# Tanh on features in PSUM, three banks for gate and up, the last three pairs pre-added, and new places

## The chip, the cores and the metric

The kernel runs on one core of one Trainium2 chip (trn2). The metric is the device time of one launch in microseconds (us), as the median of several runs. The core has TensorE (matrix products into PSUM), VectorE, ScalarE (one table function per instruction), GpSimd and SyncE; each engine works through its own instructions in order, and semaphores keep the engines apart.

## The reference

Two layers of a gated model on x (8 batches x 512 rows x 256 columns) and a context of 64 rows per batch. Cut to what matters:

```python
# layer 0: attention over 64 context rows, then a mixture of experts (8 experts, the best 2 of each row, and a shared one)
x = x + tanh(g_xattn[0]) * attention(layernorm(x), ctx, side)
x = x + tanh(g_ffn[0]) * (expert(ln, shared) + sum_e cw[e] * expert(ln, e))   # expert: silu(x Wg) * (x Wu) @ Wd
# layer 1: additive attention, then a quantized linear layer
h   = tanh(txt_proj[:, None, :, :] + feat_proj[:, :, None, :] + b)            # 8 x 512 x 64 x 256
rho = einsum('bftd,d->bft', h, w)
att = softmax(rho masked); txt_h = att @ text
w_s, b_s = tanh(txt_h @ Wcw + bcw), tanh(txt_h @ Wcb + bcb)
x = x + tanh(g_xattn[1]) * (w_s * layernorm(x) + b_s)
x = x + tanh(g_ffn[1]) * (round_and_clip(layernorm(x) / s) * s @ (ternary - 1) + bias)
```

The Tanh over 8 x 512 x 64 x 256 elements is the largest work of ScalarE, the experts that of TensorE.

## The kernel before

**Stages.** First each batch goes through attention, normalization, routing and a scatter of its rows by expert into DRAM, while TensorE also works on the shared expert of batches 0 to 4 (units of kind shared). Then come 71 tiles of 128 routed rows and, among them, 12 tiles of kind own, which are the shared expert on the rows of batches 5 to 7. A tile, called a unit, has these steps: fetch (SyncE loads its rows and 1.5 MB of weights), turn_rows (TensorE transposes the rows), gate and up (TensorE, a PSUM bank each), gate_act (ScalarE's Silu of gate, then VectorE's product with up, which gives act), narrow (TensorE, into bank 5, which VectorE copies out). From the moment that a batch's rows are complete, they are gathered, added to x and normalized (mix_in), and TensorE makes two products feature(b, 0) and feature(b, 1), one for each half of the 256 columns, 128 x 512 each.

**Pairs.** For each batch there are 32 pairs (b, m), each of two text rows. A pair needs Tanh of the features plus a text column, 2 x 2 times 128 x 512 elements. A pair is either done alone, in four ScalarE instructions that add the text column as bias (L748), or it is added first: VectorE makes the four sums (preadd, L1124 and L1125) and ScalarE runs one Tanh of 2048 columns (L737). PAIRS says how many of a batch's 32 pairs are added. On some pairs, as many as JOINS says, VectorE folds the lower half into the upper (join, L1131), and TensorE's sum of the pair (L1484, 32 output columns, into bank 6) has half as many products. Eight pair buffers rotate: a pair's buffer is free when the sum of the pair eight before is done. After 32 pairs, mix_out: rho is read, turned, softmaxed, and the linear layer follows (turn_q, linear 0 and 1).

**Order.** Each stage has a place on a common line of time units: a batch's 32 pairs take 64 units, a routed tile 8, a pair 2. Each engine's order is by place plus its own lag from LAGS. PLACES holds the places of chains, as "opened", the listing of which tiles are opened (a chain of small VectorE instructions, L1018 to L1035), of sum, join and preadd. Only the order follows from it; the times are what semaphores make of it. The tail is what comes after the last tile, from the middle of batch 6 on.

**Banks.** Gate and up of unit n stand in banks 2(n%2) and 2(n%2)+1, the shared expert's narrow in bank 4, rows in 5, rho in 6. All other products rotate through a pool (function count): banks 7, 5 and 6 while routing runs, 7 and 4 among the tiles, more in the tail. The features are among these: VectorE copies them from their bank to featT in SBUF (L1114), and before it does so it waits for the last Tanh of the batch before that reads featT. Preadd and the alone Tanhs read featT:

```python
read = [m for m in range(T // 2) if b and not plan.added(b - 1, m)]
if read:
    e.wait_ge(s_wide, pair_of(b - 1, read[-1]) + 1)
...
e.tensor_copy(featT[ec], bank[:, :]).then_inc(done, 1)
```

Line numbers of the rows: L1287 gate and up, L1292 those of the shared expert, L1411 turn_rows, L1458 narrow, L1466 feature, L1484 sum, L1516 linear, L1386 turn_odds on TensorE; L728 Silu of gate, L667 copies out of PSUM, L718 and L699 work of routing on ScalarE; L1242 linear, L958 sigmoid on VectorE.

## Time and profile before

| | |
|---|---|
| time, median of 3 runs | 1027.43 us (1023.06 to 1028.69) |
| profiled execution, span | 1025.4 us |
| TensorE (PE) busy | 934.7 us, 91% |
| its weight loads (PEld) | 742.7 us, 72% |
| VectorE (DVE) busy | 748.9 us, 73% |
| ScalarE (ACT) busy | 674.1 us, 66% |
| GpSimd (POOL) busy | 219.0 us, 21% |
| moved by DMA | 218.68 MB, mean 213 GB/s |

The span is that of the profiled execution, from its first to its last instruction; the time of a run is measured from outside. How to read it: busy shares are means over stages with different limits. ScalarE is 66% busy in all but almost idle up to 360 us. A matmul's end is modelled, so a busy TensorE need not be at its peak; what tells more is whether one group of matmuls starts as the one before ends. In a group "x24" 24 records stand together; an f32 product is recorded as two.

### The profile page before, as it was taken

To read this page: it belongs to the slowest core of one execution; us is meant where nothing else is said; L and a number is where in the kernel's file an instruction comes from. 1 tells how busy PE (TensorE), PEld (TensorE's weight loads), DVE (VectorE), ACT (ScalarE), POOL (GpSimd) and SP (SyncE) were. 2 spreads that over 40 slices of the span, in tenths; PEclk is the share of its full clock that TensorE was granted. 3 is DMA by queue.
4 is the path that set the end of the run, shared out by engine and by line. 5 is a ranking of instruction groups with operands and counts; after the bars stand their busy time and mean duration, and the time that the engine had idled before them with its cause. 6 is when DMAs were issued, how large, how long until landed. Compare 5 with 4: busy or idle time off the path is not lost. (4 is left out here: it accounts for less than half of the span.)

```text
span 1025.4 us, 22330 instructions
## 1 busy us (share of the span) xinstructions
PE 934.7 (91%) x8078; PEld 742.7 (72%) x8078; DVE 748.9 (73%) x1959; ACT 674.1 (66%) x983; POOL 219.0 (21%) x250
## 2 busy tenths in 40 slices
PE   8689999989988799999999999999999999985773
PEld 5557887779988787777777878888888887842331
DVE  3787988862222389978869869868876997795995
ACT  2122222201100069999999999989997998899992
POOL 1014543540112222312212211202211211220000
PEclk9579999999998899999999999999999999989886
DMA  7826677948996866756756667768777776410000
GB/s 247 338 62 236 244 267 283 351 174 279 331 338 227 272 232 226 236 165 219 237 175 228 211 202 253 267 219 277 266 253 231 268 260 220 149 32 12 2 22 21
DMA packets 137456, 218.68 MB, mean 213 GB/s; under 512 B 14113, under 2 KB 79138, under 8 KB 137346
## 3 DMA queue, kind: packets, MB, share of 16 engines
q1 hardware_dynamic: 119202, 156.55, 45.9%
q10 hardware_dynamic: 8592, 34.60, 8.7%
q0 software_dynamic: 9552, 26.10, 7.2%
q8 instruction: 65, 1.06, 0.4%
q14 instruction: 45, 0.37, 0.1%
HBM read 159.14 MB, written 58.06 MB: 212 GB/s over the span
## 5 line engine op out<-in xcount | busy, mean ns | idle before, releaser
L1287 PE MATMUL bank<-rowsT,expert_w 128*128 128x128 f32 x2656 | 328.3, 278 | 0.5 <-DVE rowsT L1053 0.5
L1287 PEld LDWEIGHTS bank<-rowsT,expert_w 128*128 128x128 f32 x2656 | 319.1, 194 | 9.5 <-issue 5.1
L748 ACT ACTIVATE tanhs<-shared_w,txtT 128x512 f32<-128x512 f32 x276 | 174.3, 718 | 24.5 <-issue 18.4
L748 ACT ACTIVATE arena<-shared_w,txtT 128x512 f32<-128x512 f32 x272 | 172.1, 720 | 0.0
L1458 PE MATMUL bank<-expert_w,act 128*128 128x256 f32 x664 | 162.4, 388 | 0.0
L1458 PEld LDWEIGHTS bank<-expert_w,act 128*128 128x128 f32 x664 | 121.7, 193 | 30.6 <-issue 17.3
L728 ACT ACTIVATE act<-bank 128x512 f32<-128x512 f32 x83 | 48.9, 589 | 114.2 <-PE bank L1287 114.2
L643 POOL DMA_DIRECT2D rows_by_expert<-rows_out x71 | 42.0, 592 | 371.4 <-DVE rows_out L1082 349.2
L654 POOL DMA_INDIRECT picked<-rows_by_expert,slot_of x64 | 75.9, 1186 | 157.6 <-issue 93.9
L1484 PE MATMUL bank<-arena,pick_w 128*32 128x256 f32 x1200 | 79.2, 389 | 3.2 <-ACT arena L737 2.3
L1484 PE MATMUL bank<-tanhs,pick_w 128*32 128x256 f32 x1112 | 74.4, 412 | 7.3 <-ACT tanhs L737 4.7
L1082 DVE COPY rows_out<-bank 128x256 f32<-128x256 f32 x71 | 29.8, 420 | 68.8 <-PE bank L1458 68.8
L633 POOL DMA_INDIRECT rows_by_expert<-arena,slot_of x64 | 63.2, 987 | 69.7 <-DVE slot_of L1003 53.2
L1292 PE MATMUL bank<-tanhs,shared_w 128*128 128x256 f32 x320 | 77.8, 392 | 0.0
L1131 DVE SCALAR_TENSOR_TENSOR tanhs<-tanhs,ratio 128x1024 f32<-128x1024 f32 x53 | 67.1, 1278 | 1.8 <-ACT tanhs L748 1.8
L1292 PEld LDWEIGHTS bank<-tanhs,shared_w 128*128 128x128 f32 x320 | 60.7, 197 | 9.9 <-issue 2.2
L748 ACT ACTIVATE normT<-shared_w,txtT 128x512 f32<-128x512 f32 x96 | 61.4, 721 | 0.0
L1484 PEld LDWEIGHTS bank<-tanhs,pick_w 128*32 128x32 f32 x1112 | 34.2, 117 | 37.0 <-issue 8.7
L1484 PEld LDWEIGHTS bank<-arena,pick_w 128*32 128x32 f32 x1200 | 35.6, 111 | 32.9 <-ACT arena L737 6.9
L1060 DVE TENSOR_TENSOR act<-act,bank 128x512 f32<-128x512 f32 x83 | 56.3, 678 | 1.6 <-ACT act L728 1.6
L1104 DVE SCALAR_TENSOR_TENSOR x<-picked,share,x 128x256 f32<-128x256 f32 x64 | 30.7, 480 | 34.6 <-DMA picked<-rows_by_expert,slot_of 33.8
L1053 DVE COPY rowsT<-bank 128x256 f32<-128x256 f32 x83 | 34.8, 419 | 28.1 <-PE bank L1411 28.0
(257 smaller groups left out, 1392.1 us busy)
## 6 DMA issues: line engine op xcount, KB each, us to landing
expert_w<-in_WgT SPq DMA_DIRECT2D x71, 512.0 KB, 3.9
expert_w<-in_WuT SPq DMA_DIRECT2D x71, 512.0 KB, 5.2
expert_w<-in_WdT SPq DMA_DIRECT2D x71, 512.0 KB, 6.9
rows_by_expert<-tanhs ACTq DMA_DIRECT2D x8, 4096.0 KB, 14.3
rows_in<-rows_by_expert SPq DMA_DIRECT2D x71, 128.0 KB, 6.1
rows_by_expert<-rows_out POOLq DMA_DIRECT2D x71, 128.0 KB, 5.6
expert_w<-in_WgsT SPq DMA_DIRECT2D x12, 512.0 KB, 3.8
expert_w<-in_WusT SPq DMA_DIRECT2D x12, 512.0 KB, 4.6
```

Source lines behind the costliest of these rows:

```text
L633: e.indirect_dma_start(out=rows_dram, out_offset=bass.IndirectOffsetOnAxis(ap=slot_of[j][:, ST * b + i:ST * b + i + 1], axis=0), in_=held[ ...
L643: e.dma_start(rows_dram[bass.ds(tile * P, P), :], rows_out[r % OUTS][:, :]).then_inc(s_stored[r % OUTS], 16)
L654: e.indirect_dma_start(out=picked[u % PICKED][:, :], out_offset=None, in_=rows_dram, in_offset=bass.IndirectOffsetOnAxis(ap=slot_of[j % 2] ...
L728: e.activation(act[n % 2][:, :], banks[2 * (n % 2)][:, :], ACT.Silu).then_inc(s_tanh, 1)
L748: got = e.activation(tiles[ec][:, S * j:S * (j + 1)], featT[ec], ACT.Tanh, bias=txtT[:, ec, t + j:t + j + 1])
L1053: e.tensor_copy(rowsT[r % 2][:, :], row_bank[:, 0:D]).then_inc(s_row_bank, 1)
L1060: e.tensor_tensor(h[:, :], h[:, :], bu[:, :], ALU.mult).then_inc(s_h, 1)
L1131: e.scalar_tensor_tensor(out=high, in0=low, scalar=ratio[:, 0:1], in1=high, op0=ALU.mult, op1=ALU.add).then_inc(s_joined, 1)
L1287: got = e.matmul(bank[:, i * P:(i + 1) * P], w[:, at:at + P], t[:, c * P:(c + 1) * P], start=c == 0, stop=c == DC - 1)
L1292: got = e.matmul(bank[:, i * HALF:(i + 1) * HALF], shared_w[:, at:at + P], norm_of(b)[:, c * S + h * HALF:c * S + (h + 1) * HALF], start=c ...
L1458: got = e.matmul(row_bank[:, 0:D], act[n % 2][:, c * P:(c + 1) * P], w[:, at:at + D], start=c == 0, stop=c == IC - 1)
L1484: got = e.matmul(rho_bank[32 * j:32 * j + 32, 0:H], pick_w[:, ec, 31 - m:63 - m], halves_of[q % PAIR][ec][:, j * H:(j + 1) * H], start=(ec ...
```

## The change

ScalarE's alone Tanhs read the features in PSUM, in banks 3 and 4 (feat_bank), where TensorE writes them; VectorE still copies them to featT, for the preadds, and the new semaphore s_feat counts these copies. Both the preadds and a batch's first alone Tanh wait for it. TensorE's feature product waits for the copy of the batch before and for that batch's last alone Tanh; VectorE's copy no longer waits for Tanhs. To free bank 3, gate and up of the tiles rotate through banks 0 to 2: unit n's up takes the bank that gate of n-1 had, and waits for that unit's Silu. Among the tiles all other products but the features use bank 7 alone. In batches 0 to 6 the last three pairs are always added, and PAIRS counts over the other 29. PAIRS, JOINS, PLACES and LAGS have new numbers. What is computed doesn't change. The diff, with the tables of lags cut:

```diff
--- before.py
+++ after.py
@@ -33,33 +33,38 @@
 
 ENGINES = ("sync", "gpsimd", "scalar", "vector", "tensor")
 
-PLACES = {"shared": -2.5, "zeroed": 62.5, "gap": 0, "opened": 25.5, "att_norm": 120, "att_norm_long": 30.5, "attend": 90,
-          "attend_long": 23.5, "moe_norm": 62, "moe_norm_long": 28, "route": 28, "route_long": 34, "late": -59, "gather": 4.5,
-          "norm": 2, "add": 7, "mix_in_end": -0.5, "join": 6.5, "sum": 5, "preadd": 4, "mix_out": 9.5, "mix_out_end": 49}
-
-
-PAIRS = {0: 18, 1: 9, 2: 12, 3: 0, 4: 0, 5: 0, 6: 13, 7: 27}
-JOINS = {0: 16, 1: 8, 2: 6, 3: 28, 4: 24, 5: 28, 6: 1, 7: 0}
+PLACES = {"shared": -2.5, "zeroed": 85, "gap": 0, "opened": 34, "att_norm": 120, "att_norm_long": 30.5, "attend": 90,
+          "attend_long": 23.5, "moe_norm": 62, "moe_norm_long": 28.5, "route": 28.5, "route_long": 33.5, "late": -59.5,
+          "gather": 2.5, "norm": 4, "add": 7, "mix_in_end": -0.5, "join": 7, "sum": 6, "preadd": 3, "mix_out": 10,
+          "mix_out_end": 48.5}
+
+
+LAST = 3
+PAIRS = {0: 16, 1: 6, 2: 6, 3: 0, 4: 0, 5: 0, 6: 11, 7: 28}
+JOINS = {0: 16, 1: 11, 2: 11, 3: 27, 4: 27, 5: 27, 6: 1, 7: 0}
 
 
 WARM = {"start": 14, "turn_rho": 2, "turn_q": 4, "linear": 0}
 
 
 LAGS = {
-    "sync": {"fetch": -21, "load_side": -5.5, "narrow": 0.5},
...
-    "scalar": {"gate_act": 1, "soft_rho": -0.5, "softmax": -1, "spread": -2, "squash": 2, "tanh": 1, ("turn", "att"): -0.5,
...
-               ("aggr", "moe"): -0.5, "apply": 2.5, "choice": -1, "convert": -16.5, "gate_act": 2.5, "join": -1, "larger": -9,
-               "linear": 3.5, "narrow": 1.5, ("newton", "att"): -2, ("newton", "lin"): -1.5, ("newton", "mix"): 0.5,
-               ("newton", "moe"): 1, "opened": 1.5, "pads": -1, "place": -0.5, ("power", "att"): -0.5, ("power", "lin"): 1,
...
-    "tensor": {"count": 2, "feature": -0.5, "larger": -2, "logits": -2.5, "narrow": 0.5, "scores": -1.5, "spread": 3, "sum": -1,
-               "text": -1, ("turn", "att"): -1, "turn_e": -3.5, "turn_rho": -3, "up": -1, "weigh": -0.5},
+    "sync": {"fetch": -16.5, "keep": 11, "linear": 4.5, "load_late": -9, "load_shared": 16, "load_side": -6.5, "load_x": -2.5,
...
+    "scalar": {"gate_act": -0.5, "logits": -2.5, "soft_rho": -0.5, "softmax": -0.5, "spread": -3, "squash": 2, "tanh": 1.5,
...
+               "apply": 1, "convert": -16.5, "count": -1, "feature": 1.5, "gate_act": 2.5, "join": -1, "larger": -7,
+               "linear": 3.5, "logits": -4, "narrow": 1.5, ("newton", "att"): -2.5, ("newton", "lin"): 1.5,
+               ("newton", "mix"): 0.5, ("newton", "moe"): 1, "opened": 0.5, "pads": -1, "place": -1, ("power", "att"): -1,
...
+    "tensor": {"convert": 1, "count": 2, "feature": 0.5, "larger": -2, "linear": 3, "logits": -1.5, "narrow": 0.5,
+               "scores": -1.5, "spread": 3, "sum": -1, "tiles": -1, ("turn", "att"): 0, ("turn", "mix"): -1, "turn_e": -1,
+               "turn_odds": 0.5, "turn_q": 0.5, "turn_rho": -4, "weigh": -0.5},
 }
 
 
@@ -175,8 +180,13 @@
 
     def added(self, b, m):
 
-        pairs, share = self.T // 2, int(PAIRS[b])
-        return m * share // pairs != (m + 1) * share // pairs
+        last = LAST if b < self.B - 1 else 0
+        pairs, share = self.T // 2 - last, int(PAIRS[b])
+        return m >= pairs or m * share // pairs != (m + 1) * share // pairs
+
+    def alone(self, b):
+
+        return [m for m in range(self.T // 2) if not self.added(b, m)]
 
     def joined(self, b, m):
 
@@ -270,7 +280,7 @@
         self.shared_no.append(h)
         self.row_no = {s: i for i, s in enumerate(
             s for s in self.of["tensor"] if s[0] == "turn_rows" or s[0] == "narrow" and self.units[s[1]][0] != "shared")}
-        self.misc = {}
+        self.misc, self.feature_turn = {}, {}
         self.after_units, freed = {}, []
         turns, uses = 0, [0] * 8
         pool, at = [7, 0, 1, 2, 3, 4, 5, 6], -1
@@ -282,14 +292,17 @@
                 pool, at = [7, 5, 6], -1
                 self.before_shared = list(uses)
             if s[0] == "routed":
-                pool, at = [7, 4], -1
+                pool, at = [7], -1
                 self.before_routed = list(uses)
-                freed = [4]
             if s[0] == "tail":
-                pool, at = [7, 4, 0, 1, 2, 3, 5], -1
-                freed += [0, 1, 2, 3, 5]
+                pool, at = [7, 0, 1, 2, 5], -1
+                freed += [0, 1, 2, 5]
             own = expand.get(s[0], [s] if s[0] in users or s[0] == "turn" else [])
             for u in own:
+                if u[0] == "feature":
+                    turns += 1
+                    self.feature_turn[u[1:]] = turns
+                    continue
                 at += 1
                 bank = pool[at % len(pool)]
                 uses[bank] += 1
@@ -410,6 +423,16 @@
 
         banks = [ctx.enter_context(nc.psum_tensor(f"bank{i}", [P, 512], F32)) for i in range(8)]
         shared_bank, row_bank, rho_bank = banks[4], banks[5], banks[6]
+        feat_bank = banks[3:5]
+        FIRST = plan.shared_units
+
+        def gate_bank(n):
+
+            return banks[2 * (n % 2)] if n < FIRST else banks[2 * (n - FIRST) % 3]
+
+        def up_bank(n):
+
+            return banks[2 * (n % 2) + 1] if n < FIRST else banks[(2 * (n - FIRST) + 1) % 3]
 
 
         rows_dram = nc.dram_tensor("rows_by_expert", ((ABSENT + 8) * P, D), F32, kind="Internal").ap()
@@ -443,6 +466,7 @@
         s_shared_mm, s_x_shared = sem("shared_product"), sem("x_shared_added")
         s_added = sem("x_expert_added")
         s_wide_in, s_wide, s_sum = sem("wide_added"), sem("wide_tanh"), sem("rho_product")
+        s_feat = sem("features_copied")
         s_joined, s_larger, s_swapped = sem("wide_joined"), sem("larger_ready"), sem("features_swapped")
         s_rho, s_rho_sub, s_rho_e = sem("rho_read"), sem("rho_less_max"), sem("rho_exp")
         s_ws, s_squash, s_affine, s_applied = sem("weighed"), sem("squashed"), sem("affine_ready"), sem("x_affine")
@@ -725,9 +749,9 @@
                         else:
                             e.wait_ge(s_shared_mm, shared_no[n - 2] + 1)
                     if by_rows(n):
-                        e.activation(act[n % 2][:, :], banks[2 * (n % 2)][:, :], ACT.Silu).then_inc(s_tanh, 1)
+                        e.activation(act[n % 2][:, :], gate_bank(n)[:, :], ACT.Silu).then_inc(s_tanh, 1)
                     else:
-                        e.activation(act[n % 2][:, :], banks[2 * (n % 2)][:, :], ACT.Tanh, scale=0.5).then_inc(s_tanh, 1)
+                        e.activation(act[n % 2][:, :], gate_bank(n)[:, :], ACT.Tanh, scale=0.5).then_inc(s_tanh, 1)
                 elif name == "tanh":
                     b, m = k
                     q = pair_of(b, m)
@@ -736,16 +760,15 @@
                         e.wait_ge(s_wide_in, wide_in_no[b, DC - 1, m] + 1)
                         e.activation(wide_pair[q % PAIR], wide_pair[q % PAIR], ACT.Tanh).then_inc(s_wide, 1)
                     else:
-                        if m == 0:
+                        if m == plan.alone(b)[0]:
                             for ec in range(DC):
-                                bank, use, _ = misc["feature", b, ec]
-                                e.wait_ge(s_misc[bank], use)
+                                e.wait_ge(s_feat, DC * b + ec + 1)
                         if q >= PAIR:
                             e.wait_ge(s_sum, q - PAIR + 1)
                         t = b * T + 2 * m
                         for ec in range(DC):
                             for j in range(2):
-                                got = e.activation(tiles[ec][:, S * j:S * (j + 1)], featT[ec], ACT.Tanh, bias=txtT[:, ec, t + j:t + j + 1])
+                                got = e.activation(tiles[ec][:, S * j:S * (j + 1)], feat_bank[ec][:, :], ACT.Tanh, bias=txtT[:, ec, t + j:t + j + 1])
                         got.then_inc(s_wide, 1)
                 elif name == "soft_rho":
                     b, = k
@@ -918,7 +941,7 @@
                 elif name == "turn" and k[0] == "mix":
                     kind, b, h = k
                     if h == 0 and b:
-                        e.wait_ge(s_misc_mm, misc["feature", b - 1, 1][2])
+                        e.wait_ge(s_misc_mm, plan.feature_turn[b - 1, 1])
                     bank, done = product(("turn", *k))
                     e.tensor_copy(turned(mixT, h), bank[:, :].rearrange("p (i c n) -> p i c n", i=2, c=DC)).then_inc(done, 1)
                 elif name == "scores":
@@ -1053,7 +1076,7 @@
                     e.tensor_copy(rowsT[r % 2][:, :], row_bank[:, 0:D]).then_inc(s_row_bank, 1)
                 elif name == "gate_act":
                     n, = k
-                    h, bg, bu = act[n % 2], banks[2 * (n % 2)], banks[2 * (n % 2) + 1]
+                    h, bg, bu = act[n % 2], gate_bank(n), up_bank(n)
                     e.wait_ge(s_tanh, n + 1)
                     if by_rows(n):
                         e.wait_ge(s_up, n + 1)
@@ -1105,19 +1128,15 @@
                                            in1=xi, op0=ALU.mult, op1=ALU.add).then_inc(s_added, 1)
                 elif name == "feature":
                     b, ec = k
-                    bank, done = product(("feature", b, ec))
-                    read = [m for m in range(T // 2) if b and not plan.added(b - 1, m)]
-                    if read:
-                        e.wait_ge(s_wide, pair_of(b - 1, read[-1]) + 1)
-                    if wide_in_no and b and plan.added(b - 1, T // 2 - 1):
+                    e.wait_ge(s_misc_mm, plan.feature_turn[b, ec])
+                    if b:
                         e.wait_ge(s_wide_in, wide_in_no[b - 1, DC - 1, T // 2 - 1] + 1)
-                    e.tensor_copy(featT[ec], bank[:, :]).then_inc(done, 1)
+                    e.tensor_copy(featT[ec], feat_bank[ec][:, :]).then_inc(s_feat, 1)
                 elif name == "preadd":
                     b, ec, m = k
                     q = pair_of(b, m)
                     w = halves_of[q % PAIR][ec]
-                    bank, use, _ = misc["feature", b, ec]
-                    e.wait_ge(s_misc[bank], use)
+                    e.wait_ge(s_feat, DC * b + ec + 1)
                     if q >= PAIR:
                         e.wait_ge(s_sum, q - PAIR + 1)
                     t = b * T + 2 * m
@@ -1254,10 +1273,8 @@
                 if use > 1:
                     e.wait_ge(s_misc[bank], use - 1)
                 if key in plan.after_units:
-                    if bank in (0, 1, 2, 3):
+                    if bank in (0, 1, 2):
                         e.wait_ge(s_h, len(units))
-                    elif bank == 4:
-                        e.wait_ge(s_x_shared, 2 * OWN)
                     elif bank == 5:
                         e.wait_ge(s_row_bank, len(row_no))
                 return banks[bank]
@@ -1422,16 +1439,20 @@
                             e.wait_ge(s_shared_w, 48)
                         for h in range(2):
                             e.wait_ge(s_misc[misc["turn", "moe", g, h][0]], misc["turn", "moe", g, h][1])
-                    if n >= 2:
+                    if n in (FIRST, FIRST + 1):
+                        e.wait_ge(s_h, n)
+                    elif n >= 2:
                         e.wait_ge(s_h, n - 1)
                     else:
                         for i in (2 * n, 2 * n + 1):
                             if plan.before_shared[i]:
                                 e.wait_ge(s_misc[i], plan.before_shared[i])
-                    up_down(n, banks[2 * (n % 2)], 0, s_gate)
+                    up_down(n, gate_bank(n), 0, s_gate)
                 elif name == "up":
                     n, = k
-                    up_down(n, banks[2 * (n % 2) + 1], N1, s_up)
+                    if n > FIRST:
+                        e.wait_ge(s_tanh, n)
+                    up_down(n, up_bank(n), N1, s_up)
                 elif name == "narrow":
                     n, = k
                     kind, g, s, j = units[n]
@@ -1459,7 +1480,15 @@
                         got.then_inc(s_rows_mm, 1)
                 elif name == "feature":
                     b, ec = k
-                    bank = product(("feature", b, ec))
+                    bank = feat_bank[ec]
+                    if b:
+                        e.wait_ge(s_feat, DC * (b - 1) + ec + 1)
+                        if plan.alone(b - 1):
+                            e.wait_ge(s_wide, pair_of(b - 1, plan.alone(b - 1)[-1]) + 1)
+                    elif ec == 0:
+                        e.wait_ge(s_h, FIRST)
+                    else:
+                        e.wait_ge(s_x_shared, 2 * OWN)
                     for h in range(2):
                         e.wait_ge(s_misc[misc["turn", "mix", b, h][0]], misc["turn", "mix", b, h][1])
                     for c in range(DC):
```

## Rows read from the trace of the kernel before

**Rows 1.** Stretches: length, then busy us (xinstructions) of PE, PEld, DVE, ACT, POOL; PEclk, DMA share, GB/s.

```profile
363.10:435.60 72.50, 69.65 (x690) 55.50 (x688) 65.27 (x139) 68.08 (x80) 19.30 (x17) 1.00 0.69 232
435.60:591.80 156.20, 154.44 (x1641) 121.20 (x1637) 124.83 (x297) 152.19 (x215) 31.78 (x36) 1.00 0.62 207
591.80:859.60 267.80, 267.04 (x2480) 224.27 (x2476) 215.46 (x403) 255.99 (x429) 49.46 (x54) 1.00 0.75 250
859.60:904.60 45.00, 44.60 (x436) 34.52 (x432) 33.75 (x80) 37.95 (x54) 7.71 (x9) 1.00 0.41 132
904.60:1004.40 99.80, 68.01 (x867) 30.78 (x866) 81.23 (x218) 99.77 (x98) 4.90 (x5) 0.86 0.05 16
```

**Rows 2.** Timeline of TensorE in batch 1: start us, length us, group.

```profile
442.88 1.95 PE L1287 MATMUL bank<-rowsT,expert_w 128*128 128x128 f32 x16
444.76 1.50 PE L1484 MATMUL bank<-arena,pick_w 128*32 128x256 f32 x24
446.08 0.61 PE L1484 MATMUL bank<-normT,pick_w 128*32 128x256 f32 x8
446.51 1.05 PE L1484 MATMUL bank<-shared_w,pick_w 128*32 128x256 f32 x16
```

**Rows 3.** Timeline of PE, DVE and ACT at the turn to batch 5.

```profile
769.31 1.99 PE L1466 MATMUL bank<-mixT,feat_w 128*128 128x512 f32 x4
...
772.92 1.88 PE L1466 MATMUL bank<-mixT,feat_w 128*128 128x512 f32 x4
...
774.84 0.69 DVE L1114 COPY shared_w<-bank 128x512 f32<-128x512 f32 x1 [0.89 <-PE bank L1466]
...
775.61 5.02 ACT L748 ACTIVATE tanhs<-shared_w,txtT 128x512 f32<-128x512 f32 x8 [6.62 <-issue]
```

**Rows 4.** Timeline of ACT in the tail: pair 12 of batch 6, last pair of all.

```profile
898.16 1.90 ACT L737 ACTIVATE arena<-arena 128x2048 f32<-128x2048 f32 x1
...
1002.53 1.90 ACT L737 ACTIVATE shared_w<-shared_w 128x2048 f32<-128x2048 f32 x1
```

**Rows 5.** Timeline of ACT in batch 0: an alone pair, a Silu, an added pair.

```profile
407.08 2.57 ACT L748 ACTIVATE tanhs<-shared_w,txtT 128x512 f32<-128x512 f32 x4
409.53 0.59 ACT L728 ACTIVATE act<-bank 128x512 f32<-128x512 f32 x1
410.01 1.92 ACT L737 ACTIVATE arena<-arena 128x2048 f32<-128x2048 f32 x1
411.81 2.57 ACT L748 ACTIVATE arena<-shared_w,txtT 128x512 f32<-128x512 f32 x4
```

**Rows 6.** Timeline of ACT while routing runs: PSUM inputs back to back.

```profile
63.81 0.36 ACT L718 ACTIVATE odds<-bank,router_b 128x128 f32<-128x128 f32 x1
64.06 0.60 ACT L699 ACTIVATE arena<-bank 128x512 f32<-128x512 f32 x1
```

**Rows 7.** Timeline of DVE in batch 1: a join, two of a pair's four preadds.

```profile
442.34 1.28 DVE L1131 SCALAR_TENSOR_TENSOR normT<-normT,ratio 128x1024 f32<-128x1024 f32 x1
443.54 0.48 DVE L1124 TENSOR_SCALAR arena<-shared_w,txtT 128x512 f32<-128x512 f32 x1
443.93 0.48 DVE L1125 TENSOR_SCALAR arena<-shared_w,txtT 128x512 f32<-128x512 f32 x1
```

**Rows 8.** Timeline of ACT and PE in batch 4: a Silu, a later up.

```profile
704.34 0.57 ACT L728 ACTIVATE act<-bank 128x512 f32<-128x512 f32 x1
...
708.06 1.95 PE L1287 MATMUL bank<-rowsT,expert_w 128*128 128x128 f32 x16
```

**Rows 9.** Timeline of PE and DVE: the linear layer's two products and their read.

```profile
747.90 0.60 PE L1516 MATMUL bank<-tern_w,out_work 128*128 128x256 bf16 x4
...
750.07 0.60 PE L1516 MATMUL bank<-tern_w,out_work 128*128 128x256 bf16 x4
...
750.61 0.87 DVE L1242 SCALAR_TENSOR_TENSOR x<-bank,scal,x 128x256 f32<-128x256 f32 x2
```

**Rows 10.** Timeline of PE and DVE at the last batch's routing.

```profile
204.40 0.30 PE L1386 MATMUL bank<-ident,odds 128*128 128x128 f32 x1 [0.58 <-ACT odds L718]
...
207.29 0.39 DVE L1035 TENSOR_REDUCE opened<-opening 128x1 f32<-128x224 f32 x1
207.59 0.18 DVE L958 TENSOR_SCALAR prob<-bank 128x32 f32<-128x32 f32 x1
```

16 lines of the change are left out of this document (9 added, 7 removed).

## The prediction

> **What bounds the kernel now.** I read the table of stretches first, because the page's shares mix stages with different limits. The reader is to see three stages in it. From 363.1 to 859.6 us, while expert tiles and feature pairs run side by side, TensorE is busy 491.1 of 496.5 us and ScalarE 476.3 [rows 1]: both look full, so the table alone does not say which sets the pace. Two timelines do. On TensorE each group starts where the one before lets go (24 records of a sum take 1.32 us, the next group starts in the same instant) [rows 2]. On ScalarE there are gaps: the longest, 6.62 us, lies ahead of batch 5's first Tanh, and behind it stand TensorE's second feature product at 772.92 and VectorE's copy of it at 774.84 [rows 3]. So where gate and up tiles run, TensorE sets the pace, closely followed by ScalarE; from about 905 us TensorE is 68% busy and ScalarE 99.77 of 99.80 us [rows 1]: there ScalarE alone is the bound. The last Tanh ends at 1004.4 [rows 4], and 21 us of one batch's softmax, normalization and linear layer follow, which the change leaves as they are.
>
> **The change part by part.**
> 1. *Tanh from PSUM.* Four Tanhs of a pair that isn't pre-added take 9.53-7.08 = 2.45 us, 0.613 each; a wide Tanh over a pre-added pair takes 1.80 [rows 5]. In both the input lies in SBUF. 512 elements cost 0.427 us at the rate that the wide one shows (1.80 less some 0.09 for 2048), so a narrow one with a bias operand pays 0.186 beside its elements. With a PSUM input the trace has two forms: Silu without a bias operand, 410.01-409.53 = 0.48 us for 512 elements [rows 5], 0.05 over its elements where the wide Tanh from SBUF pays 0.09; and Exp with a bias operand, 64.06-63.81 = 0.25 us for 128 [rows 6], 0.143 over its elements where the narrow Tanh pays 0.186. Both say 0.04 us less per instruction. Bounds are 0 and 0.05; I take 0.04, the row of the nearest form. A pair costs 4 x 0.57 = 2.28 us.
> 2. *Which pairs are pre-added.* PAIRS over 29 pairs and three more make 19, 9, 9, 3, 3, 3, 14 and 28: 88 for 79. ScalarE's Tanh work falls from 177 x 2.45 + 79 x 1.80 = 575.9 us to 168 x 2.28 + 88 x 1.80 = 541.4, by 34.5 us. VectorE gains nine pre-adds of four 0.40 us [rows 7] (14 us) and nine joins (111 to 120) of 1.20 [rows 7] (11 us): it goes from 82% to some 87% of the stage [rows 1], beside other work.
> 3. *Where ScalarE's 34 us go.* With the pairs of the diff and the Silus of each stretch, ScalarE needs 68, 73, 73, 77, 78 and 78 us for batches 0 to 5, 447 us in all. TensorE is busy for 491.1 us there [rows 1] and loses none of its tiles. So nearly all of it turns into idle time of ScalarE. What TensorE itself sheds is the joins': an unjoined pair is 16 records, 0.88 us by 1.32 for 24 [rows 2], a joined one half of that; nine more joined pairs, all before the tail, save 9 x 0.44 = 4.0 us. Of TensorE's 5.4 us idle in that stage [rows 1] I count 0.5 as regained, since its waits are for rows and not for Tanhs.
> 4. *The tail.* From pair 12 of batch 6, at 898.16, to the end ScalarE never waits [rows 4]. There are 20 pairs of batch 6 (11 narrow, 9 wide) and 32 of batch 7 (5 and 27). With the new lists they are 10 and 10, 4 and 28: (16 x 2.45 + 36 x 1.80) - (14 x 2.28 + 38 x 1.80) = 104.0 - 100.3 = 3.7 us. Ahead of pair 12 ScalarE can gain little, since pair 12 needs its buffer back from the sums of pairs 4 to 7; I add 0.8. Together 4.5.
> 5. *Up waits for Silu.* With three banks, up of unit n writes where gate of n-1 stood, and waits for Silu n-1. Behind it on TensorE stand narrow n-1 and the next sums. In the tightest unit that I found the Silu starts at 704.34 and ends at 704.9, and the up product that would wait starts at 708.06 [rows 8]: 3.1 us to spare, and the new places move Silu two units of place (over 2 us) ahead of the Tanhs. Cost 0; if that cover is gone, the wait lasts one pair of Tanhs at most, 2.3 us.
> 6. *Features wait on TensorE.* The products now need the last narrow Tanh of the batch before (pair 26 to 28), and all behind them waits too. Three wide Tanhs, 5.4 us, lie between that pair and the batch's end. At the turn to batch 5 ScalarE had done its last Tanh 6.62 us ahead of 775.61, at 769.0, and pair 28 three pairs of 2.45 us before, at 761.6: 7.7 us ahead of the features at 769.31 [rows 3]. Cost 0 to 1 a batch, 0 taken. In exchange VectorE's copy waits no more for Tanhs, but the first Tanh still waits for both copies, so the gap ahead of a batch stays.
> 7. *One bank for the rest.* Banks 3 and 4 go to the features; turns, rho and the linear layer rotate in bank 7 alone. The second linear product starts 2.17 us after the first, and VectorE reads the first at 750.61, after the second has begun at 750.07 [rows 9]. It would now wait for that read to end, 0.87 us later: 1.4 us. The new places bring the product three units closer to its read, so I take 0.3 a batch, 2.0 in all with the like of it; bounds 0 and 3 us in each of six batches.
> 8. *Places before the tiles.* The first long listing of opened tiles on VectorE ends at 207.6 and delays the last batch's sigmoid to 207.59, whose input was there at 204.7 [rows 10]. Placed 9.5 units earlier (8.5 by PLACES, 1 by its lag) it leaves that 2.9 us free, and the tile stage starts that much sooner. Loads and zeroing move too, with no row that prices them: bounds -5 and +3, I take -2.5.
>
> **Sum**, against the profiled span of 1025.4 us: -2.5 - 4.0 - 0.5 - 4.5 + 2.0 = -9.5, so 1015.9. The median of the runs is 2.0 above that span, and I keep this: **1018 us**, its own range 1009 to 1024.
>
> **The rivals.**
> *A: ScalarE sets the pace throughout.* For it: 476 us busy of 496.5 [rows 1]. Then the full 34.5 us come off, less the 5 or so that TensorE's tiles still force: 1027.4 - 2.5 - 29 = 996. For it too: TensorE's weight loads fill only 224.3 of 267.8 us in batches 3 to 5 [rows 1]. Against it: TensorE's records follow each other without a wait [rows 2], its loads are short of the span because those of the sums have 32 columns, and it is ScalarE that has gaps [rows 3]. The Trainium skill ("Perfetto Trace Analysis", Identifying the Most-Contended Engine) says that matmul busy time is a bad metric, because matmuls are pipelined, and that busy time of the weight loads is a good one. By that rule TensorE would have some 16% of room there, and the time would be this rival's; the timeline speaks against it. 7%.
> *B: bank 7 costs more than it frees (slower).* VectorE's queue is fuller by 25 us and in order; if it reads the first linear product later than 1.6 us after its end, TensorE stands, and with it every tile, because the products sit between tiles. At 3 us in each of six batches: 1025.4 - 11.5 + 18 + 2.0 = 1034. For it: the read now comes after the second product [rows 9]. Against it: VectorE waits for TensorE at the features too [rows 3], so its queue is not late. 15%.
> *C: the PSUM input gives nothing to Tanh.* The tail gains 1.3 for 3.7 us and batches 1 and 2 need 77.1 us of ScalarE each (23 x 2.45 + 9 x 1.80 + 4.5 for the rest) where TensorE, at half of 154.4 [rows 1] less its joins, needs 75.5: 1018 + 2.4 + 2 = 1022. Only rows of other functions speak against it. 10%.
> *D: the start doesn't gain or loses*, by loads that come later: 1018 + 2.5 to 5.5, about 1022. 12%.
>
> **How the numbers follow.** 56% for the forecast, 7, 15, 10 and 12% for the rivals. A measurement of this kernel tells some 0.5% from no change, 5.1 us: faster is below 1022.3, slower above 1032.6. Faster: 54 + 7 + 3 (part of C) = 64%; same: 2 + 7 + 10 = 19%; slower: 15 + 2 (the worst of D) = 17%. The range leaves out A, and the upper half of B: 1007 to 1032.
>
> **What would show it.** Right: narrow Tanhs 2.28 us a pair; TensorE still without gaps in batches 1 to 5, and ScalarE's gaps grown to some 5 to 13 us a batch; pair 12 of batch 6 to the end about 102 us; 21 us behind the last Tanh as before. Wrong: TensorE waits ahead of the linear products, the features or up (steps 5 to 7), a narrow pair of 2.45 us (step 1), batches on TensorE shorter by more than their joins (A), or a tile stage that doesn't start 2 to 3 us sooner (step 8).

## The result, and the profile after

The changed kernel is not faster: its median is 1030.0 us (18 runs, 1026.2 to 1035.0), that of before, run beside it, 1023.8 (18 runs). Ratio **1.0054** (95% interval 1.0034 to 1.0073), slower by 6 us where the prediction had it faster by 9.5. On a later chip it was 1.0035 (1.0007 to 1.0064). The time itself lies in the range of 1007 to 1032. The profiled execution spans 1029.8 us, against 1025.4.

The table of stretches of the kernel after, cut at the same events as [rows 1] (columns as there):

```profile
363.66:442.31 78.65, 71.50 (x690) 57.00 (x688) 65.64 (x140) 66.81 (x78) 17.71 (x17) 0.98 0.64 215
442.31:593.06 150.75, 150.75 (x1584) 119.36 (x1580) 128.28 (x294) 147.00 (x225) 33.77 (x36) 1.00 0.63 213
593.06:868.13 275.07, 268.64 (x2464) 223.41 (x2460) 232.34 (x444) 241.60 (x403) 48.78 (x54) 0.99 0.72 245
868.13:905.60 37.47, 37.47 (x359) 29.91 (x355) 26.73 (x55) 29.69 (x43) 5.67 (x7) 1.00 0.43 145
905.60:1008.80 103.20, 72.81 (x945) 34.67 (x943) 91.79 (x252) 103.17 (x100) 7.26 (x7) 0.90 0.05 17
```

The tile stage begins at 363.7 us (363.1 before). Batches 1 and 2 are 5.5 us shorter than in [rows 1], batch 0 6.2 us longer, batches 3 to 5 7.3 longer: 8.0 us lost in the stage, 4.1 won from the first feature product of batch 6 to the end (165.8 to 161.7 us). TensorE is busy for about what it was (490.9 for 491.2 us of the six batches) but idle for 13.6 instead of 5.4.

The list of TensorE's waits tells where. Engine, line, what was waited for, us in total, times, longest. Before, from 363.1 to 859.7:

```profile
PE bank L1411 <- DVE rows_out L1082: 4.3, 5, 1.2
PE bank L1336 <- DVE normed L916: 0.7, 1, 0.7
```

and after, from 363.7 to 868.1 (L1428 is L1411 of before, L1105 is L1082, the copy of a unit's rows out of PSUM; L1098 adds a shared unit's rows to x):

```profile
PE bank L1428 <- DVE rows_out L1105: 10.0, 4, 4.0
PE bank L1428 <- DVE x L1098: 2.1, 3, 0.7
PE bank L1353 <- DVE normed L939: 1.2, 1, 1.2
```

TensorE can't turn the next rows until VectorE has copied the last ones out of the same bank. The longest of these waits, batch 3, in the timeline of VectorE and then TensorE:

```profile
612.13 0.48 DVE L1127 SCALAR_TENSOR_TENSOR x<-picked,share,x 128x256 f32<-128x256 f32 x1 [0.99 <-DMA picked<-rows_by_expert,slot_of]
612.53 0.49 DVE L1163 TENSOR_TENSOR rhos<-bank,maskadd 128x128 f32<-128x128 f32 x2
616.51 0.48 DVE L1127 SCALAR_TENSOR_TENSOR x<-picked,share,x 128x256 f32<-128x256 f32 x1 [3.48 <-DMA picked<-rows_by_expert,slot_of]
616.91 1.28 DVE L1150 SCALAR_TENSOR_TENSOR arena<-arena,ratio 128x1024 f32<-128x1024 f32 x1
618.11 0.42 DVE L902 BATCH_NORM_STATS2 ln_mix_stats<-x 128x6 f32<-128x256 f32 x1
618.44 1.27 DVE L1150 SCALAR_TENSOR_TENSOR arena<-arena,ratio 128x1024 f32<-128x1024 f32 x1
619.63 0.41 DVE L1173 TENSOR_REDUCE sm_rmax<-rhos 128x4 f32<-128x256 f32 x1
620.07 0.42 DVE L1174 TENSOR_TENSOR rhos<-rhos,sm_rmax 128x256 f32<-128x256 f32 x1
620.42 0.42 DVE L1105 COPY rows_out<-bank 128x256 f32<-128x256 f32 x1
...
620.98 0.66 PE L1428 MATMUL bank<-ident,rows_in 128*128 128x128 f32 x2 [4.04 <-DVE rows_out L1105]
```

The add at L1127 is at the head of VectorE's queue, and the gathered rows that it adds aren't there: 0.99 and 3.48 us. Behind it stand two joins, the statistics, the row maximum and a subtraction, and only then the copy that TensorE needs. In the kernel before the same piece reads:

```profile
612.90 0.48 DVE L1104 SCALAR_TENSOR_TENSOR x<-picked,share,x 128x256 f32<-128x256 f32 x1 [0.61 <-DMA picked<-rows_by_expert,slot_of]
613.30 1.28 DVE L1131 SCALAR_TENSOR_TENSOR arena<-arena,ratio 128x1024 f32<-128x1024 f32 x1
614.50 0.41 DVE L1154 TENSOR_REDUCE sm_rmax<-rhos 128x4 f32<-128x256 f32 x1
614.94 0.42 DVE L1155 TENSOR_TENSOR rhos<-rhos,sm_rmax 128x256 f32<-128x256 f32 x1
615.28 0.42 DVE L1082 COPY rows_out<-bank 128x256 f32<-128x256 f32 x1
```

with no wait of TensorE behind it. By the new places and lags the gather is asked for at 5.5 instead of 4.5 units of place and its adds come at 11.5 instead of 13: 6 units apart instead of 8.5. One more join and the statistics have also come between the second add and the copy.

The wait costs more than its own length. Behind it the clock that TensorE was granted stood at half its speed, and 16 records of gate or up (L1304) took 3.07 us where they had taken 1.95:

```profile
615.00 1.95 PE L1304 MATMUL bank<-rowsT,expert_w 128*128 128x128 f32 x16
...
621.43 3.07 PE L1304 MATMUL bank<-rowsT,expert_w 128*128 128x128 f32 x16
```

The stretch behind the wait of 3.49 us in batch 0 shows the same in its column PEclk, 0.50 (1.2 instead of 2.4 GHz):

```profile
388.40:391.50 3.10, 3.08 (x15) 3.10 (x16) 3.10 (x6) 1.97 (x2) 0.57 (x1) 0.50 0.62 221
```

These two stretches, 3.4 us each, are the 0.98 and 0.99 in the table; before has 1.00 in all six batches [rows 1]. They are why TensorE is as busy as before although it has 72 records fewer.

### The profile page after: what moved, and what is told of

Read it like the earlier page. It is cut to its first block and busy times, and to the rows that moved or that the text cites. A ratio compares the mean times of both kernels' runs of the same rounds, so it can differ in the third digit from the quotient of the medians.

```text
span 1029.8 us, 22228 instructions
## 1 busy us (share of the span) xinstructions
PE 932.3 (91%) x8006; PEld 741.2 (72%) x8006; DVE 773.8 (75%) x2004; ACT 648.3 (63%) x956; POOL 219.4 (21%) x250
## 5 line engine op out<-in xcount | busy, mean ns | idle before, releaser
L1304 PE MATMUL bank<-rowsT,expert_w 128*128 128x128 f32 x2656 | 332.4, 279 | 2.0 <-DVE act L1083 1.5
L1304 PEld LDWEIGHTS bank<-rowsT,expert_w 128*128 128x128 f32 x2656 | 320.9, 195 | 15.8 <-issue 10.8
L771 ACT ACTIVATE tanhs<-bank,txtT 128x512 f32<-128x512 f32 x296 | 184.1, 833 | 26.2 <-DVE shared_w L1134 26.2
L1479 PE MATMUL bank<-expert_w,act 128*128 128x256 f32 x664 | 160.3, 384 | 0.0
L771 ACT ACTIVATE arena<-bank,txtT 128x512 f32<-128x512 f32 x240 | 149.5, 850 | 0.0
L752 ACT ACTIVATE act<-bank 128x512 f32<-128x512 f32 x83 | 58.7, 707 | 125.7 <-PE bank L1304 125.6
L1105 DVE COPY rows_out<-bank 128x256 f32<-128x256 f32 x71 | 29.8, 420 | 73.9 <-PE bank L1479 73.9
L761 ACT ACTIVATE arena<-arena 128x2048 f32<-128x2048 f32 x36 | 72.0, 2107 | 1.8 <-DVE arena L1144 1.8
L1127 DVE SCALAR_TENSOR_TENSOR x<-picked,share,x 128x256 f32<-128x256 f32 x64 | 30.6, 478 | 35.3 <-DMA picked<-rows_by_expert,slot_of 34.8
```

The lines of the kernel that those rows point to most:

```text
L752: e.activation(act[n % 2][:, :], gate_bank(n)[:, :], ACT.Silu).then_inc(s_tanh, 1)
L761: e.activation(wide_pair[q % PAIR], wide_pair[q % PAIR], ACT.Tanh).then_inc(s_wide, 1)
L771: got = e.activation(tiles[ec][:, S * j:S * (j + 1)], feat_bank[ec][:, :], ACT.Tanh, bias=txtT[:, ec, t + j:t + j + 1])
L1304: got = e.matmul(bank[:, i * P:(i + 1) * P], w[:, at:at + P], t[:, c * P:(c + 1) * P], start=c == 0, stop=c == DC - 1)
L1479: got = e.matmul(row_bank[:, 0:D], act[n % 2][:, c * P:(c + 1) * P], w[:, at:at + D], start=c == 0, stop=c == IC - 1)
```

## The experiments

The theory: **the adds come too soon behind their gather**, and the change's own terms are as predicted. The rivals: the other new places, VectorE's load of pre-adds and joins, bank 7, or Tanh from PSUM are to blame. The ratio is always to the kernel before on the same chip.

**Adds later, alone, in the kernel after.**

```diff
-    "vector": {"add": 2,
+    "vector": {"add": 3.5,
```

> The changed kernel with one number altered: VectorE's lag of add is 3.5 and not 2, so that the adds of gathered rows stand at 13 units, where the kernel before had them, and the gathers stay at the changed places. Theory (the adds stand too close behind their gathers, VectorE waits for the gather's transfer and the copy of a row tile behind it comes late, so TensorE's turn_rows waits): the waits of 3.5 and 4.0 us ahead of turn_rows in batches 0 and 3 go, and the time falls by 6 to 10 us to 1020 to 1024. Rival (VectorE's 25 us of added work hold its queue up): the waits stay or move to other tiles, the time stays within 2 us of 1030. Rival (bank 7, up's wait or the features' wait on TensorE): also within 2 us of 1030.

Measured 1.0016 (1.0000 to 1.0033). The waits shrink (3.11 us in batch 0, 2.22 in batch 3) but stay: 4 us of the loss, less than the 6 to 10 expected.

**Gather, norm and add as before, in the kernel after.**

```diff
-"gather": 2.5, "norm": 4
+"gather": 4.5, "norm": 2
-    "gpsimd": {"gather": 3, "narrow": 1,
+    "gpsimd": {"narrow": 1.5,
-    "vector": {"add": 2,
+    "vector": {"add": 1.5,
```

> The changed kernel with the places and lags of gather and add as before (gather at 4.5 with no lag, add at 11.5 plus 1.5, norm 2, GpSimd's lag of narrow 1.5). Theory of the early adds: as the run with the late add or up to 2 us better, 1018 to 1023, TensorE's stretch from batch 0's features to batch 7's falls from 577.3 to some 568 us. Rivals (VectorE's load, bank 7, the waits on TensorE): 1028 to 1032.

Measured 0.9977 (0.9952 to 1.0003). These few numbers are worth 8 us. The granted clock stays at 1.00 in the six batches, and TensorE, with the same products as in after, is busy 488.1 us for 490.9: 2.7 us of the 8 were the slow clock behind the waits.

**The same numbers of after, put into the kernel before.**

> The kernel before with the changed places and lags of gather and add (gather at 2.5 with GpSimd's lag 3, add at 9.5 plus 2, norm 4, GpSimd's lag of narrow 1), and nothing else of the change. Theory of the early adds: it becomes slower by 5 to 10 us, with waits of several us ahead of turn_rows in batches 0 and 3. Rival (it takes the fuller VectorE queue of the change for the adds to hurt): slower by at most 3 us. If the adds play no part: no change.

Measured 1.0154 (1.0133 to 1.0175), span 1038.0: 14 us between the medians, 16 by the ratio, with nothing of the mechanics changed. TensorE waits 3.56 us for the copy in batch 3, as in after, and 3.23 in batch 0, and behind these waits the clock is at 0.50 for 6.8 and 3.4 us: TensorE is busy 496.1 us in the six batches for 491.2. VectorE waits for gathered rows 26 times instead of 15:

```profile
DVE x L1104 <- DMA picked<-rows_by_expert,slot_of: 55.7, 26, 5.4
```

This is the cause, shown from both sides, and larger than the 5 to 10 us expected. How much belongs to the gather and how much to the adds isn't told apart; the adds alone gave 4 of the 8 us in after. (The norm's number only makes up for the gather's: gather, add and norm sum to 13.5 in both kernels, so its chain stays where it was.)

**Both: gather and norm as before, and the adds 1.5 later than before.**

```diff
-    "vector": {"add": 2,
+    "vector": {"add": 3,
```

> The kernel after with gather and norm where before has them and the adds 1.5 units of place later than before (4.5 + 8.5 and 10.0 apart). If the adds that wait for the gather's transfer at the head of VectorE's queue are what makes TensorE wait at the turn of rows in batches 0 and 3: those waits (2.0, 1.6 and 2.1 us with gather, norm and add old) shrink to under 1 us each, and the time falls 2 to 4 us below that of the kernel with these three old, to 1020 (0.995 of before). Rival, VectorE is simply full there: no change from 0.998.

Measured **0.9937** (0.9913 to 0.9961), 1018.5 us, and on another chip 0.9935 (0.9914 to 0.9956), 1017.5 us: faster than both kernels. TensorE's wait for the copy is 2.8 us in all on the second chip, where after has 10.0, and none of it lies in batch 3 on the first.

**How much of that is the later adds'?** The kernel before with the adds alone 1.5 later:

> The kernel before with its adds 1.5 units of place later, nothing else. If the gain of the better version is the change's own (fewer joins' work on TensorE, a faster tail) and the later adds only undo the new places: before's waits for rows in batches 0 and 3 shrink by 1 to 5 us, so 0.996 to 0.999, above 0.9937. If the gain is the later adds alone: 0.994 or less.

It came from a chip on which before takes 1050 us: 0.9948 (0.9917 to 0.9980). So both once more, side by side on one chip:

> The kernel before with its adds 1.5 later, beside the better version on the same chip. By TensorE's stretches (from the first feature product to the end: 662.7 us here against 662.3 and 665.1 in the two profiles of before, 656.5 in the better version) the later adds are worth 0 to 2.5 us in before and the change's own terms some 6: then 0.9975 to 1.000 on a chip where before takes 1024, 0.995 on the slower one. If all of the better version's gain is the later adds: 0.994.

> The better version (the kernel after with gather and norm as before, adds 1.5 later than before) again, on the same chip: 0.9937, and 4 to 6 us below the kernel before with the later adds if the shares, the Tanh from PSUM and the faster tail are its own gain; equal to it if they aren't.

Measured 0.9986 (0.9961 to 1.0011) and 0.9935 (0.9914 to 0.9956): 1022.7 and 1017.5 us. The later adds may give before 1 us; 5 us are the change's own on this chip. On the slower one the pair is not told apart by its times: 0.9948 for before with later adds, 0.9932 (0.9900 to 0.9964) for the better version with the front of before, whose run follows below. The six batches, first before with later adds, then the better version:

```profile
358.31:851.80 493.49, 491.13 (x4803) 400.86 (x4801) 405.57 (x838) 477.28 (x724) 99.16 (x107) 1.00 0.70 236
```
```profile
356.58:852.10 495.52, 488.50 (x4730) 396.86 (x4728) 427.44 (x876) 455.28 (x704) 101.23 (x107) 1.00 0.70 235
```

TensorE has 73 records fewer and is busy 2.6 us less, but idles 7.0 us instead of 2.4: the stage isn't shorter at all. The gain that the traces show stands behind it, 166.2 to 161.7 us, where ScalarE alone is the bound.

**Is Tanh from PSUM worth anything?** The kernel after with the alone Tanhs reading the copy in SBUF:

```diff
-got = e.activation(tiles[ec][:, S * j:S * (j + 1)], feat_bank[ec][:, :], ACT.Tanh, bias=txtT[:, ec, t + j:t + j + 1])
+got = e.activation(tiles[ec][:, S * j:S * (j + 1)], featT[ec], ACT.Tanh, bias=txtT[:, ec, t + j:t + j + 1])
```

> The changed kernel with the narrow Tanhs reading the copy in SBUF (featT) and not PSUM; banks, waits and places as changed. By the prediction's step 1 a narrow pair takes 2.45 us again for 2.28, which counts in the tail alone (14 narrow pairs, 2.4 us) and a little in batches 1 and 2: slower than the changed kernel by 2 to 5 us. Rival (the PSUM input hurts, since the records of Tanh and Silu end later in the changed kernel, 0.8 to 1.1 us after their start for 0.72): faster than the changed kernel by 2 us or more.

Measured 1.0137 (1.0112 to 1.0162), 8 us above after. The timeline of ScalarE, first this kernel, then after (an alone pair and the added one behind it):

```profile
373.22 2.56 ACT L771 ACTIVATE tanhs<-shared_w,txtT 128x512 f32<-128x512 f32 x4
375.67 1.90 ACT L761 ACTIVATE arena<-arena 128x2048 f32<-128x2048 f32 x1
```
```profile
372.65 2.45 ACT L771 ACTIVATE tanhs<-bank,txtT 128x512 f32<-128x512 f32 x4
374.93 1.97 ACT L761 ACTIVATE arena<-arena 128x2048 f32<-128x2048 f32 x1
```

Start to start a pair takes 2.45 us from SBUF and 2.28 from PSUM. The loss is larger than the 2 to 5 us expected: of the spans' 7.7 us, 2.1 are in the tail, and 4.5 in batches 1 and 2, which take 77.5 and 77.8 us instead of 75.2 and 75.6: there ScalarE sets the pace without PSUM.

**The lists of before** (79 pre-added and 111 joined pairs, none always added), in the kernel after and in the better version (VectorE's copy waits for the last pair's pre-adds only where it has any):

```diff
-LAST = 3
-PAIRS = {0: 16, 1: 6, 2: 6, 3: 0, 4: 0, 5: 0, 6: 11, 7: 28}
-JOINS = {0: 16, 1: 11, 2: 11, 3: 27, 4: 27, 5: 27, 6: 1, 7: 0}
+LAST = 0
+PAIRS = {0: 18, 1: 9, 2: 12, 3: 0, 4: 0, 5: 0, 6: 13, 7: 27}
+JOINS = {0: 16, 1: 8, 2: 6, 3: 28, 4: 24, 5: 28, 6: 1, 7: 0}
```

> The kernel after with the lists of pre-added and joined pairs of before (79 and 111 instead of 88 and 120, no three pairs always added). Steps 2 to 4 of the prediction: TensorE gets nine joins' worth back, +4.0 us, and the tail two more narrow pairs, +1: about 5 us above the kernel after (1030), so 1035, with feature-to-feature work on TensorE 4 us more in batches 0 to 5. Rival, VectorE's extra 25 us of pre-adds and joins cause the new waits (those on normed in batch 0 and the 0.70 us ones of batches 3 to 5): 1026 or less, and these waits shrink.

> The better version (gather and norm as before, adds 1.5 later) with the shares of before: 79 pre-added and 111 joined pairs, no three pairs always added. Steps 2 to 4: nine joins' worth of TensorE, +4.0 us, and 1 us in the tail, so 0.9937 + 0.005 = 0.9985 of before. If also the last three pairs are what hides the features' wait for the last narrow Tanh (step 6: 0 with them): TensorE waits ahead of the feature products of every batch from 4 on, and ScalarE with it ahead of batch 7, where it alone sets the pace: 3 to 6 us more, 1.002 to 1.005.

Measured 1.0228 (1.0200 to 1.0255) and 1.0042 (1.0015 to 1.0069), both where before takes 1050. Kernels from different chips are compared from the first feature product to the end, since the time ahead of it depends on the chip: 682.3 us for 666.1 in after, 665.8 for 656.3 in the better version (with the front of before, below, on the same chip). That is 16 and 9.5 us more, where 5 were expected of the first, and of the second 5, or 9 to 12 if the features' wait came. In the first VectorE is busy 17 us less in the six batches than in after. The rival had the new waits shrink by that and the time fall. Those of 0.70 us for L1098 are gone, but the larger ones for the copy of the rows stay (9.3 us in all for 10.0), so a fuller VectorE doesn't cause them. Of the 16 us, 6.9 lie behind the six batches, where ScalarE stands for 5.67 us at the turn to batch 7. The second falls in two: six batches 4.6 us longer, and 167.2 for 162.3 behind them, because of this (TensorE, VectorE and ScalarE at the turn to batch 7):

```profile
957.27 2.82 ACT L771 ACTIVATE normT<-bank,txtT 128x512 f32<-128x512 f32 x4
959.54 2.34 ACT L761 ACTIVATE shared_w<-shared_w 128x2048 f32<-128x2048 f32 x1
...
960.19 5.37 PE L1495 MATMUL bank<-mixT,feat_w 128*128 128x512 f32 x8 [4.54 <-issue]
...
965.60 0.69 DVE L1134 COPY shared_w<-bank 128x512 f32<-128x512 f32 x1 [1.31 <-PE bank L1495]
...
966.37 1.84 ACT L771 ACTIVATE tanhs<-bank,txtT 128x512 f32<-128x512 f32 x3 [4.48 <-DVE shared_w L1134]
```

Batch 6 now has an alone pair just before its last one. Its Tanh holds the bank until 960.1, the feature product waits, and ScalarE, the bound there, has only the last added pair left and then stands for 4.48 us. The three pairs always added are what hides that wait. At the turns to batches 4 to 6 TensorE waits 0.8 to 1.3 us ahead of the feature products, and 0.3 at the turn to batch 2. The three waits for L1098 are gone here too.

**All places and lags: those of before in the kernel after, and those of after in the kernel before.**

> The kernel after with every place and lag of before, only the mechanics and the shares new. If the places of gather, norm and add are all of the new places' cost: about as with those three old alone, 1021 to 1024 (0.998 of before). If the prediction's sum holds for the mechanics (-4.0, -0.5, -4.5, +2.0) and the new places cost more than those three show: 1018 or less. Rival: the other new places are there because the mechanics need them (up behind Silu, products in one bank), so without them TensorE waits ahead of up or linear: 1030 or more.

> The kernel before with every place and lag of after. If gather, norm and add are all that costs: as with those three alone, about 1039 (1.015). If the prediction's step 8 holds (front 2.5 sooner): 1036. Rival: the other new places make good what these three lose: within 0.5% of before.

Measured, both where before takes 1050: 1.0231 (1.0200 to 1.0261) and 1.0146 (1.0107 to 1.0185). The second is what gather, norm and add alone had cost, so the other new places give before nothing. The first is the rival's case. TensorE's waits from 379.8 to 905.4:

```profile
PE bank L1541 <- DVE x L1257: 9.7, 5, 3.0
PE bank L1424 <- DVE rows_out L1101: 9.1, 8, 3.1
PE bank L1424 <- DVE x L1094: 6.6, 3, 2.2
PE bank L1509 <- DVE shared_w L1146: 3.7, 3, 1.4
```

L1541 is the linear product. The mechanics do need new places, just not those of gather and adds.

**Bank 7 alone, in the kernel before**, on two chips of the slower sort:

```diff
-                pool, at = [7, 4], -1
+                pool, at = [7], -1
```

> The kernel before with turns, rho and linear of the routed stage rotating in bank 7 alone (bank 4 unused there). Step 7 of the prediction: 0.3 us a batch, +2 us (1.002), up to 3 us a batch; the second linear product should wait some 1.4 us for VectorE's read of the first. Rival B: 3 us or more a batch, +18 (1.018). Theory now: less than 3 us in all, since after shows no wait ahead of linear.

> The kernel before with the products of the routed stage in bank 7 alone once more, on whichever chip. On the slower chip it took 1.0125 of before with waits of 1.3 to 3.0 us ahead of the second linear product in batches 1 to 5 (9.9 us) and 0.8 ahead of four second feature products, which the change doesn't have. If the chip has no part in this: 1.010 to 1.013 again, rival B's size, with the places of before. If it has: 1.002 to 1.006.

Measured 1.0125 (1.0088 to 1.0162) and 1.0135 (1.0085 to 1.0186), 13 and 14 us, where the theory had less than 3. The second's waits, from 386.9 to 898.5, and one of them:

```profile
PE bank L1516 <- DVE x L1242: 10.1, 5, 3.1
PE bank L1466 <- DVE shared_w L1114: 3.1, 4, 0.8
```
```profile
521.90 0.87 DVE L1242 SCALAR_TENSOR_TENSOR x<-bank,scal,x 128x256 f32<-128x256 f32 x2
522.82 0.61 PE L1516 MATMUL bank<-tern_w,out_work 128*128 128x256 bf16 x4 [3.06 <-DVE x L1242]
```

The second linear product waits for the read of the first in batches 1 to 5, twice 3 us and three times 1.3. With the places of after the read comes in time, as after's batch 4 shows:

```profile
755.68 0.60 PE L1545 MATMUL bank<-tern_w,out_work 128*128 128x256 bf16 x4
756.32 0.88 DVE L1261 SCALAR_TENSOR_TENSOR x<-bank,scal,x 128x256 f32<-128x256 f32 x2
758.13 0.60 PE L1545 MATMUL bank<-tern_w,out_work 128*128 128x256 bf16 x4
```

**The front.** Loads, zeroing and listing as before, in the kernel after and in the better version, with after and before profiled again beside the first:

> The kernel after with the sync queue's lags, the zeroing and the listing of opened tiles where before has them. Step 8 of the prediction: the earlier listing frees 2.9 us, so the first feature product comes 2.5 us later than in after. Theory now, from the four runs on the slower chip, where kernels with the old places reach the first feature product at 380 to 384 us and those with the new at 388 to 392: the new places of the loads lose what the earlier listing gains or more, so here 0 to 3 us sooner than after on a fast chip, 5 to 8 sooner on the slow one.

> The better version with the loads, the zeroing and the listing of tiles where before has them. In the last comparison on one chip the first feature product came at 360.7 us in after, 358.5 with these old, 357.8 in before, 357.8 in the better version: its start scatters by 3 us from run to run, so the front's places are worth nothing that can be told: 0.9937 within 0.25%. Step 8 of the prediction: 2.5 us later, 0.996.

> The kernel after once more, beside the next three on one chip. The four runs before this one came from a chip on which the kernel before takes 1050 us instead of 1024, most of it before the first feature product (380 to 392 us instead of 363). If the ratio of after to before hangs on the chip, it comes out above the 1.005 of the first measurement where before is slow; if not, 1.005 again.

> The kernel before once more, for its profile on the same chip as the other three: ratio 1.000 within 0.25%.

Measured 1.0060 (1.0038 to 1.0082), 0.9932 (0.9900 to 0.9964), 1.0035 (1.0007 to 1.0064) and 0.9978 (0.9949 to 1.0007). On that chip the first feature product came at 358.5, 360.7 and 357.8 us in the first, third and fourth, where it had been at 363.7 in after and 363.1 in before: the front's places move nothing that stands out of this scatter.

## Why the prediction was wrong, and where it was right

The terms of its sum, in us, from profiled spans: after against before (1029.8 and 1025.4), and the better version against before on one chip (1014.5 and 1022.9):

| | predicted | after - before | better version - before |
|---|---|---|---|
| start of the tile stage | -2.5 | +0.6 | +0.1 |
| TensorE busy, six batches | -4.0 | -0.3 | -2.6 |
| TensorE idle, six batches | -0.5 | +8.2 | -1.3 |
| from batch 6's features to the end | -4.5 | -4.1 | -4.5 |
| bank 7 (within the idle time) | +2.0 | 0 | 0 |
| sum | -9.5 | +4.4 | -8.4 |

That -8.4 comes close to -9.5 is in part luck. The profile of before that it is compared with holds a wait of 2.94 us for the copy in batch 3, which the first profile of before doesn't have, and the better version's adds stand later than the change has them.

- **The step that failed is the missing one.** Part 7 and part 8 took up new places where a bank or the front was concerned, but the gather and the adds were moved too, and no sentence priced them. Step 3 saw that TensorE's 5.4 us of idle time were waits for rows and forecast them to shrink by 0.5; they grew by 8.2. The row to read was VectorE's wait at 612.90 in before, 0.61 us for the gathered rows: it says that this add has no time to spare. Coming 1.5 units sooner behind a gather asked for 1 unit later, it could be expected to wait longer, and the queue behind it held the copy that TensorE needs. It was worth 8 us in after and 14 to 16 in before. A part of that is the half clock behind the long waits, which the sum doesn't have either: it hides the shed work of TensorE (-0.3 in after; -2.6 where the clock stayed up).
- **Step 1 was right**: 2.28 us a pair from PSUM for 2.45. The Trainium skill ("Perfetto Trace Analysis", Optimizing Scalar/DVE Operations) gives ScalarE a data-access overhead of some 93 ns on SBUF and 51 on PSUM; the trace agrees, with 0.17/4 = 0.043 us an instruction. The 0.09 us of overhead that step 1 takes off the wide Tanh stands in no row here; the measured 0.043 doesn't need it. Rival C held this at 2 us for batches 1 and 2 and 2.4 for the tail; the kernel with Tanhs from SBUF had 4.5 and 2.1, and its batches of 77.5 and 77.8 us are the 77.1 that C worked out.
- **Steps 2 and 3**: VectorE grew by 20.7 us in the six batches. The prediction put all 25 there, but two of the nine new pre-added pairs are in batches 6 and 7, so its own numbers make 22. TensorE sheds 2.6 us of the 4.0, seen only where the clock stayed up. What the sum didn't have is that the new lists take it back: the better version idles 4.6 us more than before with later adds. 2.1 of these are the three waits of 0.70 us at L1098, once in each of batches 3 to 5. With the lists of before, in after and in the better version, these three are gone (and waits ahead of the features come), so the lists cause them. Ahead of L1098 on VectorE stand pre-adds and joins without a gap; which of the lists' three parts (more pre-adds, more joins, the three last pairs) does it was not tried.
- **Step 4 was right**: -4.1 in after, -4.5 in the better version; 21 us behind the last Tanh as before (1008.9 to 1029.8).
- **Step 5 was right**: TensorE never waits ahead of up. **Step 6 was right** with the three pairs; without them it costs 4.5 us at one turn and 0.3 to 1.3 at others.
- **Step 7**: +2.0 was wrong both ways. With the places of before the waits are 1.3 to 3.1 us, three of the five of the size worked out there (1.4), and make 10 us in a kernel that is 13 or 14 us slower: nearer to rival B's 18; with those of after they are gone. 0.3 a batch was a value between two cases, neither of which came out at it.
- **Step 8 fell.** The listing still stands just ahead of the last batch's sigmoid on VectorE:

```profile
208.19 0.39 DVE L1058 TENSOR_REDUCE opened<-opening 128x1 f32<-128x224 f32 x1
208.49 0.18 DVE L981 TENSOR_SCALAR prob<-bank 128x32 f32<-128x32 f32 x1
```

  exactly as in [rows 10]. 9.5 units of place were taken for an earlier turn, but a place only orders VectorE's steps, and in the traces the steps ahead of the listing and behind it are the same, before and after. Put back to its old place (with the loads, in the kernel after) it stands there too.
- **Rival A** is out: ScalarE's work fell, but the stage in which it had room is no shorter in the better version (495.5 us) than in before with later adds (493.5). By the Trainium skill's rule ("Perfetto Trace Analysis", Identifying the Most-Contended Engine), that busy time of the weight loads tells TensorE's headroom, the better version would have it at 396.9 of 495.5 us, 80%, with room. The runs disagree: ScalarE's work in the stage fell from 477.3 to 455.3 us, TensorE waits for 7.0 us in all, and the stage stays as long.

## What to carry to other kernels

A change that moves steps is to be priced step by step for every step moved, first for those that wait for a transfer at the head of an in-order queue: read the wait that they have now (0.61 us here meant no reserve), and what is queued behind them. A resource taken away (a bank, a last pair's buffer) costs by where its neighbours stand: products in one bank cost 13 us with the places of before and show no wait with those of after. A wait of TensorE may cost more than its length, so its busy time and granted clock are to be read beside it. And when a large change comes out level, put its tuning numbers back group by group: this one had a gain of some 5 us, and the places of the gather and the adds hid it.
